# A decoder layer of three stages on one core: the first steps' fills, weight splits and rotation put in another order

## The reference

```python
x = layernorm(x + self_attention(x))         # causal; q and k: rms norm, then rotation (rope)
x = layernorm(x + cross_attention(x, ctx))   # causal and key mask; k and v from ctx
x = layernorm(x + ffn(x))                    # rms norm with gamma, gelu, 1024 heavy + 128 light hidden units
# q_out = [q1*cos - q2*sin, q2*cos + q1*sin], the same for k
# every one of the 256 tokens goes to the heavy branch too: top_k takes all 256 of 256
```

## Time and profile before

| | us |
|---|---|
| median of 3 runs (1009.51 to 1010.22) | 1009.86 |
| the profiled execution, its own time | 1012.33 |
| its span, first to last instruction | 1010.6 |
| PE busy / DVE busy / ACT busy / POOL busy | 911.5 / 737.3 / 498.4 / 486.2 |
| mean granted TensorE clock | 0.961 |
| chain that ended last: PE / DVE / issue / POOL | 58% / 17% / 10% / 4% |

### The profile page before, as it was taken

The page is one execution under the profiler, slowest core; times in us unless marked ns, Lnnn a source line. Parts: engine busy times, 40 slices in busy tenths (PEclk is TensorE's granted clock), DMA queues, the critical chain, the costliest instruction groups (busy, mean ns, idle before and its releaser), DMA issues.

```text
span 1010.6 us, 21915 instructions
## 1 busy us (share of the span) xinstructions
PE 911.5 (90%) x7904; PEld 709.0 (70%) x7904; DVE 737.3 (73%) x1847; ACT 498.4 (49%) x1063; POOL 486.2 (48%) x899
## 2 busy tenths in 40 slices
PE   2567888999999999999999999999999999998886
PEld 1335565787878777787878787777878786766575
DVE  8676778677778878777878788787777787563612
ACT  1132443647465555546474645556464645455343
POOL 2173454545555664645464655646455555242221
PEclk8558799999999999999999999999999999999899
DMA  3909192836657290927466381908365563805000
GB/s 106 184 16 135 26 128 33 117 43 90 81 63 108 38 134 10 130 35 109 62 86 86 53 118 27 126 21 123 48 99 73 68 92 43 117 3 68 19 1 22
DMA packets 79644, 74.24 MB, mean 73 GB/s; under 512 B 8592, under 2 KB 78896, under 8 KB 79536
## 3 DMA queue, kind: packets, MB, share of 16 engines
q1 hardware_dynamic: 75872, 68.90, 49.2%
q10 hardware_dynamic: 3664, 3.94, 1.2%
HBM read 17.49 MB, written 4.20 MB: 21 GB/s over the span
## 4 chain that ended last, share of the span: by engine, by line
PE 58%; DVE 17%; issue 10%; POOL 4%; ACT 3%; DMA 2%; SPq 2%; POOLq 0%; ACTq 0%; DVEq 0%
PE bank L347 53%; PE bank L372 4%; DVE mx L891 3%; POOL pr L1209 2%; SPq L274 2%; DVE rest L875 2%; DVE x L972 1%; DMA stk1k<-nat1k 1%; ACT pr L746 1%; DVE y L944 1%; DVE st L951 1%; DVE on L935 1%; DVE rden L928 1%; DVE ss L997 1%; DVE nat2q L880 1%
## 5 line engine op out<-in xcount | busy, mean ns | idle before, releaser
L746 ACT ACTIVATE pr<-bank 128x384 f32<-128x384 f32 x512 | 242.2, 500 | 199.0 <-PE bank L347 198.7
L891 DVE TENSOR_REDUCE mx<-bank 128x3 f32<-128x384 f32 x512 | 268.3, 552 | 88.0 <-PE bank L347 86.3
L1209 POOL TENSOR_SCALAR_AFFINE_SELECT pr<-pr 128x256 f32<-128x256 f32 x512 | 225.9, 450 | 193.6 <-ACT pr L746 190.1
L347 PE MATMUL bank<-w,g 128*128 128x256 f32 x576 | 170.8, 389 | 1.1 <-ACT g L758 1.1
L347 PE MATMUL bank<-cmaskb,idb 128*128 128x256 bf16 x512 | 144.7, 283 | 21.9 <-DVE mx L891 10.4
L758 ACT ACTIVATE g<-bank,b 128x256 f32<-128x256 f32 x144 | 68.2, 474 | 112.9 <-PE bank L347 112.4
L1233 POOL TENSOR_TENSOR xTlow<-xT,xThigh 128x512 fp32r<-128x512 f32 x16 | 21.0, 1313 | 171.6 <-ACT xThigh L682 171.6
L347 PEld LDWEIGHTS bank<-w,g 128*128 128x128 f32 x576 | 89.6, 190 | 5.2 <-ACT g L758 1.5
L347 PE MATMUL bank<-stk1k,stk1q 97*128 97x128 bf16 (+1 forms) x512 | 87.0, 256 | 0.0
L347 PE MATMUL bank<-stk1q,stk1k 100*128 100x256 bf16 (+1 forms) x512 | 80.7, 257 | 4.2 <-DMA stk1q<-mT 3.2
L347 PEld LDWEIGHTS bank<-cmaskb,idb 128*128 128x128 bf16 x512 | 49.9, 97 | 47.5 <-DVE mx L891 21.4
(11 more groups left out here) (157 smaller groups left out, 1824.9 us busy)
## 6 DMA issues: line engine op xcount, KB each, us to landing
stk1q<-nat1q SPq DMA_DIRECT2D x96, 128.0 KB, 4.5
stk1k<-nat1k SPq DMA_DIRECT2D x96, 128.0 KB, 6.5
stk2k<-nat2k SPq DMA_DIRECT2D x96, 128.0 KB, 4.6
stk2q<-nat2q SPq DMA_DIRECT2D x96, 128.0 KB, 6.1
xT<-in_xT SPq DMA_DIRECT2D x16, 256.0 KB, 7.5
ctxT<-in_ctxT SPq DMA_DIRECT2D x16, 256.0 KB, 7.6
x<-in_x SPq DMA_DIRECT2D x16, 256.0 KB, 6.8
out_x<-x SPq DMA_DIRECT2D x16, 256.0 KB, 6.9
```

Source lines behind the costliest of these rows:

```text
L347: return nc.tensor.matmul(out, lhsT, rhs, start=start, stop=stop, skip_group_check=check)
L746: nc.scalar.activation(pr[:, h % (2 * HG), :], ring_bank("T", a, b, h)[:, 0:3 * P], ACT.Exp, scale=HD ** -0.5)\
L891: V.tensor_reduce(mx3[:, h, :], scored[:, 0:3 * P].rearrange("p (k t) -> p k t", k=3), AX.X, ALU.max, negate=True).then_inc(s_mx[a], 1)
L1209: G.affine_select(out=slot, in_=slot, compare_op=ALU.is_ge, fill=0.0, base=0, pattern=[[0, 2], [1, P]], channel_multiplier=-1).then_inc(s_ ...
```

## The change

GpSimd fills the cross rows behind its first difference (step -2); the zero fill of `stk[1]` k row 96 goes behind the rotation of sequence 0 on DVE; that rotation does q of both token tiles, then k of both, and PE transposes q after the first half; the first q/k product starts on the high halves alone and waits for the low parts inside; `halve_cross` goes from the end of step -1 to step 0, behind `max_t(1, 0)`, and ACT's exponential of head 4 of sequence 0 waits for it; `scale_w1` goes from step 0 to step 1. The order of the three products of `halves_proj` changes for all sequences, their number does not.

```diff
+        def rotate_first(eng, ops, b):
+            eng.wait_ge(s_qn, TT * (b + 1))
...
+            for s in range(2):
+                for t in range(TT):
+                    qv = qn[:, t, :].rearrange(four, s=2, h=H, f=2)
+                    rv = rot[:, t, :].rearrange(four, s=2, h=H, f=2)
+                    ops.tensor_tensor(...)
+                    for half in range(2):
+                        last = ops.tensor_tensor(...)
+                last.then_inc(s_rot, 1)
+                eng.wait_ge(s_rot, TT * b + s + 1)
+                for t in range(TT):
+                    last = ops.tensor_tensor(...)
+                last.then_inc(s_rope, 1)
...
# SP, stacks
-                        sp.wait_ge(s_rows, 5)
+                        sp.wait_ge(s_rows[2], 2)
...
# PE
+            def halves_proj(out, src, t, w, low=None):
+                products = [(x, y, c) for x, y in ((src[0], w[0]), (src[1], w[0]), (src[0], w[1])) for c in range(C)]
                 for n, (x, y, c) in enumerate(products):
+                    if low and n == C:
+                        pe.wait_ge(s_xlow, 1)
+                    if low and n == 2 * C:
+                        pe.wait_ge(s_whalf, low)
...
-                pe.wait_ge(s_xlow, b + 1)
+                pe.wait_ge(s_xhigh if first(b) and t == 0 else s_xlow, b + 1)
...
             def transpose_qk1(b):
-                pe.wait_ge(s_rope, TT * (b + 1))
+                pe.wait_ge(s_rope, 1 if first(b) else TT * (b + 1))
...
                 four_transposes(SPLIT_BANK[1][0], qr[:, :, 0:D]).then_inc(s_nat[1], 1)
+                if first(b):
+                    pe.wait_ge(s_rope, TT)
...
-            pe.wait_ge(s_whalf, 2)
+            pe.wait_ge(s_whalf, 1)
...
# ACT, exponential
+                if a == 1 and first(b) and h == HG:
+                    act.wait_ge(s_chalf, 4)
...
# DVE, step
                 if starting(i + 1):
-                    rotate(dve, V, i + 1)
+                    rotate_first(dve, V, i + 1)
+                    dve.wait_ge(s_rows[1], 2)
+                    rows(1, 1, ROW_BIAS, ROW_BIAS + 1, 0.0)
...
                 if live(c):
                     max_t(2, c)
+                if first(i):
+                    halve_cross()
                 if live(i + 1):
                     split(1, i + 1, 0, 0)
...
-                if first(i):
+                if first(c):
                     scale_w1()
...
-                if first(i + 1):
-                    halve_cross()
-                    more_rows()
...
             halves(wqk1raw, wqk1, 0)
-            dve.wait_ge(s_rows, 2)
-            rows(1, 1, ROW_BIAS, ROW_BIAS + 1, 0.0)
...
# POOL, step
                 if live(i + 2):
...
+                    if first(i + 1):
+                        pool.wait_ge(s_rows[2], 2)
                     G.tensor_tensor(xTp[1][:, :, :], xT[:, :, :], xTp[0][:, :, :].bitcast(f32), ALU.subtract)\
                         .then_inc(s_xlow, 1)
+                if first(i + 2):
+                    for n, (side, hi) in enumerate(((1, K_ALL), (0, ROW_BIAS + 1))):
+                        pool.wait_ge(*((s_xlow, 1), (s_rows[2], 1))[n])
+                        G.memset(stk[2][side][ROW_BIAS:hi, :, :].bitcast(f32), two_ones).then_inc(s_rows[2], 1)
```

More of the change, by code:

```diff
@@ L159, in build @@
         s_wqk1 = sem("wqk1_loaded"); s_wself = sem("self_weights_loaded"); s_wcross = sem("cross_weights_loaded"); s_wffn = sem("ffn_weights_loaded")
-        s_const = sem("consts_ready"); s_mask = sem("keybias_step"); s_rows = sem("fixed_rows_ready")
+        s_const = sem("consts_ready"); s_mask = sem("keybias_step"); s_rows = two("fixed_rows_ready")
         s_table = sem("rope_table_step"); s_scaled = sem("ffn_weights_scaled"); s_halved = sem("w1_high_ready"); s_w1 = sem("w1_halves_ready"); s_xnhigh = sem("xn_high_ready")
@@ L239, in build @@
         h2 = HD // 2
+        two_ones = float(np.array([0x3F803F80], np.uint32).view(np.float32)[0])
         def rotate(eng, ops, b):
@@ L265, in rotate @@
                                            rot[:, t, s * D:(s + 1) * D].rearrange(pairs, c=C, d=HD), ALU.add)
+                last.then_inc(s_rope, 1)
+        def rotate_first(eng, ops, b):
+            eng.wait_ge(s_qn, TT * (b + 1))
+            four = "p (s h f d) -> p s h f d"
+            pairs = "p (j c d) -> p j c d"
+            for s in range(2):
+                for t in range(TT):
+                    qv = qn[:, t, :].rearrange(four, s=2, h=H, f=2)
+                    rv = rot[:, t, :].rearrange(four, s=2, h=H, f=2)
+                    ops.tensor_tensor(qc[:, t, s * D:(s + 1) * D].rearrange("p (h d) -> p h d", d=HD),
+                                      qn[:, t, s * D:(s + 1) * D].rearrange("p (h d) -> p h d", d=HD),
+                                      ropeC[:, t, s:s + 1, :].to_broadcast([P, H, HD]), ALU.mult)
+                    for half in range(2):
+                        last = ops.tensor_tensor(rv[:, s, :, half, :], qv[:, s, :, 1 - half, :],
+                                                 ropeS[:, t, s:s + 1, half * h2:(half + 1) * h2]
+                                                 .to_broadcast([P, H, h2]), ALU.mult)
+                last.then_inc(s_rot, 1)
+                eng.wait_ge(s_rot, TT * b + s + 1)
+                for t in range(TT):
+                    last = ops.tensor_tensor(qr[:, t, s * D:(s + 1) * D].rearrange("p (c d j) -> p j c d", c=C, d=HD),
+                                             qc[:, t, s * D:(s + 1) * D].rearrange(pairs, c=C, d=HD),
+                                             rot[:, t, s * D:(s + 1) * D].rearrange(pairs, c=C, d=HD), ALU.add)
                 last.then_inc(s_rope, 1)
@@ L353, in tok_proj @@
                 return last
-            def halves_proj(out, src, t, w):
-                products = [(x, y, c) for x, y in ((src[0], w[0]), (src[0], w[1]), (src[1], w[0])) for c in range(C)]
+            def halves_proj(out, src, t, w, low=None):
+                products = [(x, y, c) for x, y in ((src[0], w[0]), (src[1], w[0]), (src[0], w[1])) for c in range(C)]
                 for n, (x, y, c) in enumerate(products):
+                    if low and n == C:
+                        pe.wait_ge(s_xlow, 1)
+                    if low and n == 2 * C:
+                        pe.wait_ge(s_whalf, low)
                     last = mm(out, x[:, c, t * P:(t + 1) * P], y[:, c, :], n == 0, n == len(products) - 1)
@@ L383, in qk1 @@
                     pe.wait_ge(s_on[1], TT * (b - 1))
-                halves_proj(bank[QK1_BANK[t]][:, :], xTp, t, wqk1).then_inc(s_qk1, 1)
+                halves_proj(bank[QK1_BANK[t]][:, :], xTp, t, wqk1, 2 if first(b) and t == 0 else None).then_inc(s_qk1, 1)
             def v1(b):
@@ L478, in scores @@
                     if first(b):
-                        pe.wait_ge(s_rows, (None, 3, 5)[a])
+                        pe.wait_ge(s_rows[a], (None, 3, 2)[a])
                     pe.wait_ge(s_stk[a], 16 * NSTK[a] * (b + 1))
@@ L1138, in step @@
                     newton(i + 2, 2)
-                if first(i + 1):
-                    halve_cross()
-                    more_rows()
-            two_ones = float(np.array([0x3F803F80], np.uint32).view(np.float32)[0])
             def rows(a, s, lo, hi, value):
[L1145 to L1149, removed]
+                V.memset(stk[a][s][lo:hi, :, :].bitcast(f32), value).then_inc(s_rows[a], 1)
             rows(1, 1, ROW_BIAS, K_ALL, two_ones)
```

## The result

The median of 11 runs is 1003.68 us (1001.88 to 1009.52) against 1010.22 of the kernel before in 11 runs (1007.49 to 1013.84). The ratio is 0.9935, with a 95% interval of 0.9917 to 0.9952: 6.5 us less. The forecast was 3.3 less (1006.6, range 1002.4 to 1009.0): the right sign and inside the range, but half the size, and outside the 1005.0 to 1008.3 of the forecast's own case.

The account below looks back on a forecast made before the run. PE bounds the long middle (672 of 700 us busy), so the start decides. Terms: -0.4 + 0.95 + 3.7 + 1.05 - 2.0 = 3.3 us gained, giving 1006.6 us against the median; range 1002.4 to 1009.0.

Parts of the forecast that it names:

- Part 1: Front: POOL's two fills and DVE's one-input copies exclude each other, so removing the zero fill there loses 0.4 us.
- Part 2: Rotation of sequence 0, q before k: three q transfers go early, the zero fill delays the split; 0.95 us gained.
- Part 3: Ahead of the first maximum: halve_cross and the cross fills leave DVE, maximum from 46.95 to 43.25; 3.7 us gained.
- Part 4: First scores_t phase: halve_cross behind max_t is just covered, but delays ctxlow and the first selects; 0.6 us lost.
- ctxlow ends later and the first selects with it: Step 0, halve_cross beside POOL: ctxlow ends at 64.05 and delays the first selects; loss 0.6 us, ends 0 and 1.5.
- Part 5: Step 0 without scale_w1: selects take 0.42 and the third value group comes at 72.9, not 73.96; 1.7 us gained.
- Part 6: Step 1 with scale_w1: it holds head 15's select and the last value group; 2.0 us lost, between 0 and 3.6.
- cast from about 127.0: Step 1, scale_w1: DVE starts at 122.65, its cast runs from about 127.0 to 128.35, head 15's select behind it.
- case D: Step 1: subtraction stops heads 14 and 15, PE pauses 3.6 us, its clock falls; slower, 1013.2 us; chance 6%.
- Case A: Front: POOL's fills do not hold DVE, so 0.4 lost becomes 1.8 gained, 1004.4 us; chance 25%.
- C: Step 0: halve_cross's four instructions end after 65.5, exponentials 4 to 7 wait, 1 to 2 us; about 1008.6; chance 12%.
- B: Step 1: scale_w1 fits into DVE's idle 6.76 us, 2.0 us less, 1004.6 us; chance 17%.

Follow-up runs that it names:

- e3: Changed kernel with POOL's two cross-row fills waiting until DVE's root chain has begun; 1002.32 us, ratio 0.9916.
- e4: Changed kernel with the rotation of sequence 0 in the old order and both transposes behind it; 1004.01 us, ratio 0.9929.
- e6: Kernel before with only the two cross fills moved to POOL, behind DVE's roots; 1006.88 us, ratio 0.9970.
- e2: Changed kernel with halve_cross back at the end of step -1; 1003.08 us, ratio 0.9919.
- e5: Changed kernel with the two cross fills back on DVE, at the end of step -1; 1004.31 us, ratio 0.9948.
- e1: Changed kernel with scale_w1 back in step 0; 1003.92 us, ratio 0.9922.
- e10: Kernel before with only scale_w1 moved to step 1; 1008.26 us, ratio 0.9977.
- e7: Changed kernel with all three late fills on POOL behind DVE's roots and halve_cross at the end of step -1; 1002.30 us, ratio 0.9918.

## Why the prediction was right and where it was wrong

**Part 1 (forecast: 0.4 lost).** Right in mechanism, 0.4 off: wv1's cast came 0.05 earlier than before. The sum let both fills end before any mask instruction; in the run the first one came in between the fills, and the second ended 0.15 behind the second fill. The lower bound, exclusion, was the right choice, and e3 prices what the free front would have brought: 1.3 to 1.6 at the first maximum. The trace also shows the part that was taken from the Trainium skill (SBUF — State Buffer, "Who interferes with whom"): the one-input mask scaling took 1.86 beside a fill, while the two-input wqk1low took 1.23 beside the first fill and was not held. Before, beside POOL's difference, which reads, it took 2.17.

**Part 2 (0.95 gained).** Right: 1.05 at the first scores, and 0.96 when undone in e4. The reasons held too: the middle part was ready at 29.68 (28.74 + 0.94), worked out as 29.9.

**Part 3 (3.7 gained).** Right in size: 3.65 alone (e6), and 4.73 with the other two parts against 4.25 in the sum. But it is not the sum of two causes. Before, 6.5 us of DVE work stood ahead of a maximum that could have come 3.7 earlier; the fills' removal alone gives all of the 3.7, and moving halve_cross gives nothing beside it (e2). Alone in the kernel before, its 2.2 us would be worth 2.2, an estimate from the earlier trace rows that no run tests. In the changed kernel each piece can be put back without loss (e2, e5), the fills because the front gets faster by it; both together were not tried.

**Part 4 (0.6 lost).** Wrong, a mis-sized term: nothing. Exponential to stack 2 takes 9.2 to 9.5 with halve_cross in it (changed) and 9.4 without it (e2). The term that failed is "ctxlow ends later and the first selects with it". ctxlow did end later, but only 0.16 behind the first exponential (57.85 to 57.69), not 0.67 as worked out, and the first select came 0.56 behind that exponential both before (63.94 to 63.38) and here (58.25). The cover held, with room: DVE's four instructions ended 0.7 behind the first exponential, not 1.3. The first seven selects took 3.23 against 4.14 before, with the splits falling on fewer of them; that this made up for the rest is argued, not shown.

**Part 5 (1.7 gained).** Right in its stretch: 1.75 to 2.0 (e1), 2.3 to 3.0 (e10). That the whole kernel gains it is not shown: e1 and e10 show no difference in time to the kernels that they are made from.

**Part 6 (2.0 lost).** Wrong, and the largest miss: 0.6 (e1). The step that failed is "cast from about 127.0", 4.35 behind the first scaling. Each scaling was put behind a select in turn; in the run the four scalings took 2.40 together, no more than in step 0, and the cast began 3.0 behind the first (118.59 less 115.60). The select of head 15 did stand behind the cast (1.40 us from 118.90), but all this came 1.3 us earlier in the phase than worked out, and PE waited only 0.23. The other end of this part exists as well: in e3 and e10 the pause before the transposes and the clock behind it cost 2.5 to 3.4 us, as case D had it, but at another instruction, with a pause of 1.50 and not 3.6, and without a slower kernel.

**Sum.** With the measured terms: 4.7 at the first maximum, 1.75 to 2.0 for part 5, 0 for part 4, less 0.6: 5.9 to 6.1, against 6.5 between the medians. So near an agreement is in part luck, since two stretches that are in no term moved as well. On the mean of its two profiles the changed kernel leads by 4.7 at the first maximum, 7.5 at stack 2, 6.0 at load 1, 5.9 at stack 3, 6.8 at load 2 and 6.9 in the span: it loses 1.5 between stack 2 and load 1, and gains 0.9 from stack 3 to load 2, where the sum has a loss. The granted clock differs between the profiles in both; how much of it is the change is open, with two profiles of each kernel. The 9.8 of the first pair holds 1.0 from the clock at the transposes and 1.3 from the steady part.

Case A did not come, and C did not. B, scale_w1 fitting into step 1, came for 1.4 of its 2.0 us. The range held because it had room for A and B, and not because its middle was right: the misses of parts 1, 4 and 6, 0.4, 0.6 and 1.4 us, all lay on one side.

## What to carry to other kernels

Before moving a fill or a copy to GpSimd, look at what VectorE does in that stretch: a one-input copy or scaling there stops for the whole fill, so place it beside two-input or PSUM work, as e3 and e7 do. Where several pieces stand in a queue ahead of a late instruction, price them together against the time at which its input is ready, since beyond that no removal is worth anything. And with two profiles of the same kernel 1.7 to 4 us apart, compare stretches of equal clock, and leave differences of 1 us to runs.

## What the runs showed of the hardware

A short pause of TensorE can cost more than its length. Behind one of 1.50 us the granted clock was 0.50 for 3 us, with PE busy all of it, and the stretch took 2.5 to 3.4 us more than in profiles that paused 0.52 or less there and kept 1.00. Which it is can go with the phase before: in seven profiles with half clock just ahead PE stayed nearer its suppliers and paused 0.5, in the two without it 1.5. And the order in time decides a lock: xTlow started 0.02 us before the cast of wqk1high here (6.77, 6.79), and the cast took 1.79 and POOL 1.26, where before the cast was first and took 0.69, and POOL 1.67; in the second profile of the changed kernel the cast was first too (6.42) and took 0.69.
